# Routing attention of a two-layer kernel: keys on partitions for 512 queries at a time, split factors, the row maximum from its own pass

## The chip, the cores and the metric

The kernel runs on one core of a Trainium2 chip. Its metric is the device time of one execution in microseconds (us). TensorE (PE, with its weight loads PEld), VectorE (DVE), ScalarE (ACT), GpSimd (POOL) and SyncE (SP, here a DMA queue) run their own instruction streams in order and wait for each other by semaphores.

## What is computed

A tensor x of 2048 rows by 256 and a context of 1601 rows by 192 go through two layers. The first is a routing layer of one head; the second is a transformer block with self-attention (16 heads of 16), cross-attention to the same context and an MLP. The change touches the first layer:

```
tok    = context @ W_proj + b_proj                  # 1601 x 256
scores = x @ tok.T / sqrt(256)                      # 2048 x 1601
attn   = softmax(scores, axis=-1)
routed = attn @ tok                                 # 2048 x 256
ps_n, in_n = ln(x), ln(routed)
u = sigmoid([ps_n, in_n] @ W_u + b_u)
r = sigmoid([ps_n, in_n] @ W_r + b_r)
cand = tanh([r * ps_n, in_n] @ W_n + b_n)
x = ln((1 - u) * x + u * cand)
```

## The kernel before

x stands as 16 tiles of 128 rows; a chunk is four tiles (512 rows). The context has 13 key tiles, the last of 65 rows. The program has four parts in time.

**First stage** (list `stage1`). TensorE makes tok twice from ctxT, by features (`tokF`, L778) and by keys (`tokT`, L782), and the keys (`k`) and values (`v`) of the cross-attention; `norm` sums the squares of the keys by head (L753). ScalarE takes k units in three passes (`split`, L614 to L616), VectorE makes their low part (`lower_parts`, L1217).

**Routing loop** (function `l0` on each engine). Tile i has its scores made with queries on partitions: XT is the stationary operand, tokF moves, 16 recorded TensorE instructions into four PSUM banks (L827). VectorE reduces the maximum (L1323), ScalarE takes one exp over 1601 columns with its row sum (L652). TensorE turns the 13 blocks of the result (L859), ScalarE copies them out (L666), TensorE multiplies by tokT (L836). Then come per tile: the norm of the routed row and of x, a chain of about twenty short VectorE instructions (L1332 to L1349); four transposes (L869); reset and update gates (L845, L848); the candidate (L877); the blend and the output norm (L1356 to L1195); and the first norm of the second layer with two transposes (L796). In step i the loop does scores of tile i, the routed product of i-1, the gates of i-2, the output norm of i-3 and the transposes of i-4. It has 20 steps.

**Projections.** Once four tiles have passed, `qkv(stage3[n])` makes q, k and v of the self-attention for chunk n (L813, L810, L753). The tables `DENSE` and `WITHIN` put it: chunks 0, 1 and 3 run as a block of their own after steps 7, 11 and 19; chunk 2 is spread within steps 16 and 17.

**Attentions.** Self- and cross-attention with the MLP (L989 scores, L713 exp, L1006 values) follow. They start when chunk 3 is projected. Their stacked q and k parts are typed F32R: a value is split in a rounded high part and a low part, and a product of F32R operands is one recorded TensorE instruction, where one of f32 operands is two.

## Time and profile before

| | us |
|---|---|
| three runs | 1571.6, 1568.4, 1571.73 |
| their median | 1571.6 |
| the profiled execution, own time | 1572.35 |
| its span, first to last instruction | 1570.7 |
| TensorE busy | 1468.8 (94%) |
| ScalarE busy | 1072.1 (68%) |
| VectorE busy | 536.5 (34%) |
| TensorE share of the chain that ended last | 75% |

Busy time is the union of an engine's instructions. Ends of matmuls are modelled, so a distance between starts tells the pace and a duration the latency. The profiled execution is 0.75 us over the median of the runs.

### The profile page before, as it was taken

The numbers are of one execution on the slowest core, as the hardware profiler recorded it, in microseconds if no ns is written. First come the engines' busy times: TensorE is split into PE (matmuls) and PEld (weight loads), VectorE is DVE, ScalarE is ACT, GpSimd is POOL, SyncE is SP. The second block draws the span as 40 slices with busy tenths as digits, with TensorE's granted clock in tenths as the row PEclk, the third lists the DMA queues.
The fourth block names the chain that finished last, engine by engine and source line by source line (L and its number), as shares of the span: only waits on it lengthen the run. The fifth ranks groups of instructions, "written<-read, shape, count | busy, mean of one in ns | idle before, by whom it ended". The sixth has DMA issues, their size and how long they took to land.

```text
span 1570.7 us, 20677 instructions
## 1 busy us (share of the span) xinstructions
PE 1468.8 (94%) x8094; PEld 644.5 (41%) x8094; DVE 536.5 (34%) x1296; ACT 1072.1 (68%) x1297; POOL 41.7 (3%) x58
## 2 busy tenths in 40 slices
PE   8889989999867999999999999899999999999998
PEld 5467757757632222322322322232232432332346
DVE  1535545545553022230331332233232142133222
ACT  2323333333325999999999999798788797788852
POOL 2100000000001000000000000000000000000000
PEclk9999999999968999999999999899899999999999
DMA  7400010010016800010010056401000100000000
GB/s 218 171 7 7 8 57 19 8 67 5 31 53 125 139 22 11 11 40 22 11 38 13 19 77 115 102 19 61 13 12 11 35 12 11 18 18 1 2 13 14
DMA packets 36651, 64.22 MB, mean 41 GB/s; under 512 B 6464, under 2 KB 22656, under 8 KB 35808
## 3 DMA queue, kind: packets, MB, share of 16 engines
q1 hardware_dynamic: 31184, 41.40, 12.1%
q0 software_dynamic: 5360, 21.37, 3.8%
q8 instruction: 70, 1.15, 0.3%
q14 instruction: 37, 0.30, 0.1%
HBM read 40.85 MB, written 22.02 MB: 40 GB/s over the span
## 4 chain that ended last, share of the span: by engine, by line
PE 75%; ACT 17%; DVE 4%; issue 3%; DMA 1%; POOL 0%; DVEq 0%; SPq 0%; ACTq 0%; POOLq 0%
PE PS L1006 22%; PE PS L989 16%; ACT PX L713 14%; PE PS L827 6%; PE PS L836 6%; PE PS L1057 4%; PE PS L1067 3%; PE PS L1042 2%; PE PS L778 2%; PE PS L877 2%; PE PS L813 2%; PE PS L753 2%; PE PS L845 1%; PE PS L848 1%; PE PS L782 1%
## 5 line engine op out<-in xcount | busy, mean ns | idle before, releaser
L713 ACT ACTIVATE PX<-PS 128x1024 f32<-128x1024 f32 (+1 forms) x928 | 883.8, 1040 | 138.6 <-PE PS L989 87.4
L1006 PE MATMUL PS<-PX,V 128*32 128x512 f32 (+1 forms) x3712 | 501.0, 612 | 5.0 <-ACT PX L713 3.1
L989 PE MATMUL PS<-QST,stack 50*128 50x512 f32 (+1 forms) x1856 | 386.0, 473 | 20.0 <-issue 14.0
L989 PEld LDWEIGHTS PS<-QST,stack 50*128 50x128 f32 (+1 forms) x1856 | 156.3, 186 | 421.7 <-ACT PX L713 340.2
L1006 PEld LDWEIGHTS PS<-PX,V 128*32 128x32 f32 (+1 forms) x3712 | 74.1, 109 | 152.3 <-issue 126.9
L1448 DVE COPY OT<-PS 128x512 f32<-128x512 f32 x32 | 22.1, 692 | 309.6 <-PE PS L1006 308.3
L652 ACT ACTIVATE PR<-PS,small 128x1601 f32<-128x1601 f32 x16 | 25.5, 1596 | 117.0 <-DVE small L1324 117.0
L827 PE MATMUL PS<-tokF,XT 128*128 128x512 f32 (+1 forms) x256 | 93.2, 518 | 4.2 <-DVE small L1305 3.6
L836 PE MATMUL PS<-tokT,PT 128*128 128x256 f32 (+1 forms) x416 | 93.3, 382 | 0.6 <-DVE CZ L1374 0.6
L836 PEld LDWEIGHTS PS<-tokT,PT 128*128 128x128 f32 (+1 forms) x416 | 78.0, 191 | 10.6 <-issue 0.8
L659 ACT ACTIVATE TR<-PS,small 128x128 f32<-128x128 f32 x32 | 10.0, 363 | 85.8 <-PE PS L848 85.8
L827 PEld LDWEIGHTS PS<-tokF,XT 128*128 128x128 f32 x256 | 45.7, 193 | 53.3 <-issue 53.2
L1067 PE MATMUL PS<-W,HIDT 128*128 128x256 f32 x192 | 52.0, 418 | 9.8 <-ACT HIDT L699 9.8
L1057 PE MATMUL PS<-HC,W 128*128 128x512 f32 x96 | 53.2, 641 | 0.0
L1475 DVE RECIPROCAL REC<-REC 128x256 f32<-128x256 f32 x30 | 52.6, 1753 | 1.0
L1067 PEld LDWEIGHTS PS<-W,HIDT 128*128 128x128 f32 x192 | 36.9, 202 | 34.6 <-issue 30.0
L1323 DVE TENSOR_REDUCE small<-PS 128x1 f32<-128x1601 f32 x16 | 29.2, 1826 | 53.6 <-PE PS L827 53.6
L1520 DVE TENSOR_SCALAR HIDT<-PS,cols 128x512 f32<-128x512 f32 x24 | 18.0, 751 | 79.9 <-PE PS L1057 79.8
L1498 DVE TENSOR_TENSOR XH<-PS,rows 128x256 f32<-128x256 f32 x28 | 11.9, 425 | 81.6 <-PE PS L1042 81.6
L859 PE MATMUL PS<-ident,PR 128*128 128x128 f32 (+1 forms) x208 | 30.8, 290 | 8.6 <-ACT PT L666 4.7
L614 ACT ACTIVATE PARTS<-PS,cols 128x512 f32<-128x512 f32 (+1 forms) x16 | 10.3, 642 | 40.7 <-PE PS L778 24.7
L813 PE MATMUL PS<-hF,SAW 128*128 128x512 f32 x64 | 32.9, 652 | 4.4 <-ACT hF L635 4.4
(146 smaller groups left out, 1187.4 us busy)
## 6 DMA issues: line engine op xcount, KB each, us to landing
QST<-q_parts SPq DMA_DIRECT2D x192, 64.0 KB
q_parts<-PARTS POOLq DMA_DIRECT2D x16, 512.0 KB, 3.4
stack<-k_parts SPq DMA_DIRECT2D x24, 200.1 KB, 6.8
stack<-k_parts SPq DMA_DIRECT2D x18, 256.0 KB
k_parts<-KPARTS POOLq DMA_DIRECT2D x8, 512.0 KB, 3.2
v_cross<-V POOLq DMA_DIRECT2D x1, 3328.0 KB, 10.0
V<-v_cross SPq DMA_DIRECT2D x2, 1664.0 KB, 13.0
k_parts<-PARTS POOLq DMA_DIRECT2D x6, 512.0 KB, 3.2
```

Of the source, the lines that this page charges most:

```text
L713: act.activation(PX[0:kr, (2 * t + half) % 4, :, :], PS[0:kr, slot:slot + 2, :], ACT.Exp, scale=SCALE).then_inc(at["exp"], 1)
L753: ins = pe.matmul(PS[0:HEADS, bank, 0:w], headsum[:, mm, :], SQ[:, mm, 0:w], start=(mm == 0), stop=(mm == 1))
L778: ins = pe.matmul(PS[:, bank, 0:w], lhs, ctxT[:, c, n:n + w], start=(c == 0), stop=(c == 1))
L813: ins = pe.matmul(PS[:, u % 4, :], SAW[:, "qk".index(kind), c, mm * P:(mm + 1) * P], hF[:, c, n:n + w], start=(c == 0), stop=(c == 1))
L827: ins = pe.matmul(PS[:, b, 0:w], XT[:, par, c, :], tokF[:, c, n:n + w], start=(c == 0), stop=(c == 1))
L836: ins = pe.matmul(PS[:, 6, 0:D], PT[0:kr, kt, :], tokT[0:kr, kt, :], start=(kt == 0), stop=(kt == LT - 1))
L877: ins = pe.matmul(PS[:, 6, 0:D], RPS[:, c, :] if c < 2 else CF[:, par, c, :], W0[:, 2, c, :], start=(c == 0), stop=(c == 3))
L989: ins = pe.matmul(PS[0:kr, 2 * (n % LOOK) + jj, :], KST[a][lo:lo + NROW, pair, kt * P:kt * P + kr].bitcast(F32R), QST[lo:lo + NROW, pair, ...
L1006: ins = pe.matmul(PS[32 * j:32 * j + 32, 6, :], V[0:kr, kt, 2 * (g // 2 * GH + j) + g % 2, :], PX[0:kr, (2 * t + j // 2) % 4, j % 2, :], s ...
L1057: ins = pe.matmul(PS[:, 7, :], (CAWQ if kind == "u" else W1)[:, c, i * P:(i + 1) * P], HC[:, c, :], start=(c == 0), stop=(c == 1))
L1067: ins = pe.matmul(PS[:, 7, 0:D], HIDT[:, k, i * P:(i + 1) * P], W2[:, k, :], start=(k == 0), stop=(k == HID // P - 1))
L1475: ch(ve.reciprocal(part, part))
```

## The change

Scores are now made with keys on partitions, for 512 queries at a time, from the raw context: x is multiplied by W_proj first (`q_unit`), giving 192 features (the bias of tok adds the same to every key of a row and falls out of the softmax). The query features and the context are split in high and low F32R parts (QP; CHI and CLO; CN by keys). Per key tile, `l0_scores` is five F32R matmuls of 512 columns and `l0_pv` six, into two banks that gather over the 13 key tiles; the result stands by context features and is multiplied by W_proj per tile (`route`, f32, which also brings the row sum in a column of its own). tokF, tokT and the 13 transposes per tile are gone. ScalarE takes exp twice per key tile (`exps`), to F32R and to f32, and VectorE makes the low part (`lower`). The row maximum is needed ahead of the exp and comes from a pass of its own: 16 pieces per chunk (`max_piece`, two F32R matmuls of high parts alone, 128 queries by up to 512 keys), a VectorE maximum for each (`max_taken`), turned to a row (`max_rows`) and put in as one more feature.

The loop is now one of slots: `slot(k)`, 23 of them. In slot k of the first 16 stand three key tiles of chunk k // 4 (four if k is a multiple of 4, j = 0), a share of the maxima of the next chunk (none at j = 0, which has the next chunk's `q_unit` instead), and the tile work for tiles k-4 (route, hats), k-5 (gates, candidate), k-6 (finish) and k-7 (transposes). Slots 16 to 22 have tile work alone, and the projections of chunks 1 and 2 within slots 16, 17, 19 and 20.

```diff
-    stage1 = ([("tokF", n, w, mm) for n, w in pcs for mm in range(2)] + [("tokT", kt, 0, 0) for kt in range(LT)])
+    stage1 = [("v", kt, 0, 0) for kt in range(LT)]
     for i, (n, w) in enumerate(pcs):
         stage1 += [("k", n, w, mm) for mm in range(2)]
-        stage1 += [("v", kt, 0, 0) for kt in range(LT * i // len(pcs), LT * (i + 1) // len(pcs))]
+        stage1 += [("max", i * len(pcs) + p, 0, 0) for p in range(len(pcs))]
         stage1 += [("norm", i, w, 0)]
     stage1 = numbered(stage1)
...
-    DENSE = {2 * TPC - 1: 0, 3 * TPC - 1: 1, 5 * TPC - 1: 3}
-    WITHIN = {TILES: stage3[2][:MIDDLE], TILES + 1: stage3[2][MIDDLE:]}
...
+    DENSE = {10: 0, 22: 3}
+    WITHIN = {16: stage3[1][:MIDDLE], 17: stage3[1][MIDDLE:], 19: stage3[2][:MIDDLE], 20: stage3[2][MIDDLE:]}
+    SLOTS = TILES + TPC + 3
...
+    def max_share(k):
+
+        j = k % TPC
+        if j == 0 or k // TPC + 1 >= CHUNKS:
+            return []
+        first = (k // TPC + 1) * TPC * len(pcs)
+        return [first + m for m in ((0, 1, 2, 3, 4, 5), (6, 7, 8, 9, 10, 11), (12, 13, 14, 15))[j - 1]]
```


TensorE, the new functions and the slot:

```diff
+        def max_piece(m):
+
+            b, tt, p = m // (TPC * len(pcs)), m // len(pcs) % TPC, m % len(pcs)
+            n, w = pcs[p]
+            w += w % 2
+            if m == 0:
+                pe.wait_ge(S["ctx_hi"], len(CTX_PARTS))
+            if m % (TPC * len(pcs)) == 0:
+                pe.wait_ge(S["l0_q_hi"], 2 * b + 2)
+            bank, q = max_bank(m), QP[b % 2]
+            take(bank, S["l0_max_taken"], m + 1)
+            pe.matmul(PS[:, bank, 0:w], q[:, 0, tt * P:(tt + 1) * P].bitcast(F32R),
+                      CHI[:, 0, n:n + w].bitcast(F32R), start=True, stop=False)
+            pe.matmul(PS[:, bank, 0:w], q[0:HALF, 3, tt * P:(tt + 1) * P].bitcast(F32R),
+                      CHI[0:HALF, 1, n:n + w].bitcast(F32R), start=False, stop=True).then_inc(S["l0_max"], 1)
+
+        def max_rows(b):
+
+            pe.wait_ge(S["l0_negmax"], b + 1)
+            take(rows_bank(b), S["l0_shift"], b + 1)
+            for tt in range(TPC):
+                ins = pe.matmul(PS[SUM:SUM + 1, rows_bank(b), tt * P:(tt + 1) * P], sm(NEGM + tt), ident[:],
+                                start=True, stop=True)
+            ins.then_inc(S["l0_rows"], 1)
+
+        for mm in range(2):
...
+            if kt == 0:
+                pe.wait_ge(S["l0_q_lo"], 2 * b + 2)
+                pe.wait_ge(S["l0_shift"], b + 1)
+            take(n % 2, S["l0_exp"], n + 1)
+            out_ = PS[0:kr, n % 2, :]
+            pe.matmul(out_, CHI[:, 0, keys].bitcast(F32R), q[:, 0, :].bitcast(F32R), start=True, stop=False)
+            pe.matmul(out_, CHI[:, 0, keys].bitcast(F32R), q[:, 1, :].bitcast(F32R), start=False, stop=False)
+            pe.matmul(out_, CLO[:, 0, keys].bitcast(F32R), q[:, 0, :].bitcast(F32R), start=False, stop=False)
+            pe.matmul(out_, CHI[:, 1, keys].bitcast(F32R), q[:, 2, :].bitcast(F32R), start=False, stop=False)
+            pe.matmul(out_, CLO[0:SUM + 1, 1, keys].bitcast(F32R), q[0:SUM + 1, 3, :].bitcast(F32R),
+                      start=False, stop=True).then_inc(S["l0_scores"], 1)
...
+            pe.wait_ge(S["l0_lo"], n + 1)
+            if first:
+                for bank in (4, 5):
+                    take(bank, S["l0_oc"], b + 1)
+            hi, lo = PH[0:kr, n % RING, :].bitcast(F32R), PL[0:kr, n % RING, :].bitcast(F32R)
+            for bank, f, w in ((4, 0, P), (5, P, SUM + 1)):
+                c_hi, c_lo = (CN[0:kr, kt, o + f:o + f + w].bitcast(F32R) for o in (0, CW))
+                pe.matmul(PS[0:w, bank, :], c_hi, hi, start=first, stop=False)
+                pe.matmul(PS[0:w, bank, :], c_lo, hi, start=False, stop=False)
+                ins = pe.matmul(PS[0:w, bank, :], c_hi, lo, start=False, stop=last)
+            ins.then_inc(S["l0_pv"], 1)
...
+        def route(i):
+
+            b, tt = divmod(i, TPC)
+            if i == 0:
+                pe.wait_ge(S["wn_loaded"], 32)
+            pe.wait_ge(S["l0_oc"], b + 1)
+            wait(pe, S["l0_hat"], i)
+            pe.matmul(PS[:, 6, 0:D + 1], OC[:, 0, tt * P:(tt + 1) * P], WN[:, 0, :], start=True, stop=False)
+            pe.matmul(PS[:, 6, 0:D + 1], OC[0:SUM + 1, 1, tt * P:(tt + 1) * P], WN[0:SUM + 1, 1, :],
+                      start=False, stop=True).then_inc(S["l0_routed"], 1)
...
+                l0_scores(n)
+                if more:
+                    q_unit(b + 1, 0)
+                l0_pv(n - 2)
+                l0_scores(n + 1)
+                l0_pv(n - 1)
+                if g is not None:
+                    gates(g)
+                if more:
+                    q_unit(b + 1, 1)
+                l0_scores(n + 2)
+                l0_pv(n)
+                if r is not None:
+                    route(r)
+                l0_scores(n + 3)
+                if g is not None:
+                    candidate(g)
+                l0_pv(n + 1)
+                if r is not None:
+                    hats(r)
+                if h is not None:
+                    h_transposed(h)
+                return
+            ms = max_share(k)
+
+            def maxima(i):
+
+                if i < len(ms):
+                    max_piece(ms[i])
+                elif ms and i == 4:
+                    max_rows(b + 1)
+
+            l0_scores(n)
+            maxima(0)
+            l0_pv(n - 2)
+            if r is not None:
+                route(r)
+            maxima(1)
+            l0_scores(n + 1)
+            maxima(2)
+            l0_pv(n - 1)
+            if g is not None:
+                gates(g)
+            maxima(3)
+            l0_scores(n + 2)
+            maxima(4)
+            l0_pv(n)
+            if r is not None:
+                hats(r)
+            if g is not None:
+                candidate(g)
+            if h is not None:
+                h_transposed(h)
+            maxima(5)
```


ScalarE and VectorE:

```diff
+            kr = key_rows(1, n % LT)
+            act.wait_ge(S["l0_scores"], n + 1)
+            if n == 0:
+                act.wait_ge(S["v_cross_stored"], 16)
+            wait(act, S["l0_pv"], n + 1 - RING)
+            act.activation(PH[0:kr, n % RING, :].bitcast(F32R), PS[0:kr, n % 2, :], ACT.Exp, scale=SCALE0)
+            act.activation(PEXP[0:kr, n % RING, :], PS[0:kr, n % 2, :], ACT.Exp, scale=SCALE0) \
+                .then_inc(S["l0_exp"], 1)
+
+        def routed_out(b):
+
+            act.wait_ge(S["l0_pv"], LT * (b + 1))
+            wait(act, S["l0_routed"], TPC * b)
+            act.copy(OC[:, 0, :], PS[:, 4, :])
+            act.copy(OC[0:SUM + 1, 1, :], PS[0:SUM + 1, 5, :]).then_inc(S["l0_oc"], 1)
...
+            ins.then_inc(S["l0_q_lo"], 1)
+
+        def max_taken(m):
+
+            p = m % len(pcs)
+            ve.wait_ge(S["l0_max"], m + 1)
+            ve.tensor_reduce(sm(MXP + m % (TPC * len(pcs))), PS[:, max_bank(m), 0:pcs[p][1]], AX, ALU.max) \
+                .then_inc(S["l0_max_taken"], 1)
+
+        def negmax(b):
+
+            ve.wait_ge(S["l0_max_taken"], (b + 1) * TPC * len(pcs))
+            ve.tensor_reduce(sm(NEGM, TPC), sm(MXP, TPC * len(pcs)).rearrange("p (t n) -> p t n", t=TPC), AX, ALU.max,
+                             negate=True).then_inc(S["l0_negmax"], 1)
...
+        def lower(n):
+
+            kr = key_rows(1, n % LT)
+            ve.wait_ge(S["l0_exp"], n + 1)
+            ve.tensor_tensor(PL[0:kr, n % RING, :].bitcast(F32R), PEXP[0:kr, n % RING, :], PH[0:kr, n % RING, :],
+                             ALU.subtract).then_inc(S["l0_lo"], 1)
...
+            if j == 0:
+                more = b + 1 < CHUNKS
+                lower(n)
+                if more:
+                    q_lo(b + 1, 0)
+                lower(n + 1)
+                gates(g)
+                if more:
+                    q_lo(b + 1, 1)
+                lower(n + 2)
+                norms(r, f, h)
+                finish(f)
+                candidate(g)
+                lower(n + 3)
+                if k == 0:
+                    x_stats()
+                return
+            ms = max_share(k)
+
+            def maxima(i):
+
+                if i < len(ms):
+                    max_taken(ms[i])
+                elif ms and i == 4:
+                    negmax(b + 1)
+
+            lower(n)
+            maxima(0)
+            norms(r, f, h)
+            maxima(1)
+            maxima(2)
+            lower(n + 1)
+            gates(g)
+            finish(f)
+            maxima(3)
+            if j == TPC - 1:
+                maxima(4)
+            lower(n + 2)
+            if j < TPC - 1:
+                maxima(4)
+            candidate(g)
+            maxima(5)
```


SyncE loads the context in two parts of three DMAs each, the cross-attention weights, WQ and 512 columns of xT ahead of the context by keys (CN32, 1601 rows of 193 values) and the constants; each later xT chunk is one DMA. The key quarters of the self-attention, which two steps of the loop loaded before, are all loaded once slot 19 has routed tile 15. GpSimd sets ones in V a second time, after the last product of the routing, since the new tiles PH and PL lie there.

TensorE in the loop, before: one tile, from its routed product to the next tile's scores.

```order
L836 MATMUL PS<-tokT,PT 128x256 x13
L845 MATMUL PS<-CF,W_96 128x128 x8
L848 MATMUL PS<-W_96,CF 128x256 x4
L859 MATMUL PS<-ident,PR 128x128 x12
L859 MATMUL PS<-ident,PR 65x128
L869 MATMUL PS<-ident,XHS 128x128 x4
L877 MATMUL PS<-W_96,RPS 128x256 x2
L877 MATMUL PS<-W_96,CF 128x256 x2
L796 MATMUL PS<-ident,XH_97 128x128 x2
L827 MATMUL PS<-tokF,XT 128x512 x6
```


The same place in the change (slot 11; QP_87 and QP_88 are the two chunks' query parts):

```order
L1062 MATMUL PS<-CF,W_100 128x128 x8
L1065 MATMUL PS<-W_100,CF 128x256 x4
L928 MATMUL PS<-CHI,QP_88 128x66
L930 MATMUL PS<-CHI,QP_88 128x66
L1009 MATMUL PS<-QP_87,CHI 65x512
L1010 MATMUL PS<-QP_87,CHI 65x512
L1011 MATMUL PS<-QP_87,CLO 65x512
L1012 MATMUL PS<-QP_87,CHI 65x512
L1013 MATMUL PS<-QP_87,CLO 65x512
L938 MATMUL PS<-ident,small 1x128 x4
L1029 MATMUL PS<-PH,CN 128x512
L1030 MATMUL PS<-PH,CN 128x512
```


The transposes of PR are gone. Between gates and candidate now stand a key tile's scores (five rows), a piece of the next chunk's maximum (L928, L930), the turned maxima (L938) and a key tile's product.

VectorE in the same place, before: from the update gate to the next tile's maximum.

```order
L1356 TENSOR_TENSOR UZ<-PS,rows_90 128x256
L1360 TENSOR_SCALAR RPS<-TR 128x256
L1361 TENSOR_TENSOR RPS<-RPS,CF 128x256
L1366 TENSOR_SCALAR E_103<-E_103,small 128x256
L1367 TENSOR_TENSOR E_103<-E_103,rows_90 128x256
L1368 TENSOR_TENSOR X<-E_103,rows_90 128x256
L1193 BN_STATS small<-X 128x6
L1195 BN_AGGR small<-small 128x2
L1374 TENSOR_TENSOR CZ<-PS,rows_90 128x256
L1379 TENSOR_TENSOR E_103<-CD,X 128x256
L1380 SCALAR_TENSOR_TENSOR E_103<-TU,E_103 128x256
L1382 SCALAR_TENSOR_TENSOR E_103<-E_103,X 128x256
```


And in the change (slot 9), from the last instruction of the norms:

```order
L1646 TENSOR_SCALAR XH_102<-X,small 128x256
L1532 TENSOR_REDUCE small<-PS 128x1 x2
L1625 TENSOR_TENSOR PL<-PEXP,PH 128x512
L1655 TENSOR_TENSOR UZ<-PS,rows_99 128x256
L1657 TENSOR_SCALAR RPS<-TR 128x256
L1658 TENSOR_TENSOR RPS<-RPS,CF 128x256
L1666 TENSOR_SCALAR E_108<-E_108,small 128x256
L1667 TENSOR_TENSOR E_108<-E_108,rows_99 128x256
L1668 TENSOR_TENSOR X<-E_108,rows_99 128x256
L1457 BN_STATS small<-X 128x6
L1459 BN_AGGR small<-small 128x2
L1532 TENSOR_REDUCE small<-PS 128x1
```


The reduction over 1601 columns, one a tile, is gone from its place; three pieces of maximum and a low part stand among the tile work in this stretch.

TensorE after the last routed tile, before (steps 17 to 19 and chunk 3's projections begin):

```order
L845 MATMUL PS<-CF,W_96 128x128 x8
L848 MATMUL PS<-W_96,CF 128x256 x4
L813 MATMUL PS<-hF,SAW 128x512 x2
L810 MATMUL PS<-SAW,hF 128x256 x4
L753 MATMUL PS<-SQ,headsum 16x512 x2
L877 MATMUL PS<-W_96,RPS 128x256 x2
L877 MATMUL PS<-W_96,CF 128x256 x2
L796 MATMUL PS<-ident,XH_97 128x128 x6
L813 MATMUL PS<-hF,SAW 128x512 x4
L810 MATMUL PS<-SAW,hF 128x256 x4
```


And in the change (slots 20 to 22, the same projections begin):

```order
L993 MATMUL PS<-hF,SAW 128x512 x2
L990 MATMUL PS<-SAW,hF 128x256 x4
L893 MATMUL PS<-SQ,headsum 16x512 x2
L1062 MATMUL PS<-CF,W_100 128x128 x8
L1065 MATMUL PS<-W_100,CF 128x256 x4
L1072 MATMUL PS<-W_100,RPS 128x256 x2
L1072 MATMUL PS<-W_100,CF 128x256 x2
L975 MATMUL PS<-ident,XH_102 128x128 x6
L993 MATMUL PS<-hF,SAW 128x512 x4
L990 MATMUL PS<-SAW,hF 128x256 x4
```


The order within a slot is turned: projections now stand ahead of the gates. Ahead of these rows there are four more slots of tile work without scores, where the loop before had one step.

## Rows read from the trace of the kernel before

**Rows 1.** Windows of stages: us, busy us (x) of PE, PEld, DVE, ACT, POOL, clock, DMA, GB/s.
```profile
62.00:132.60 70.60, 61.66 (x271) 44.19 (x272) 34.69 (x124) 20.56 (x43) 0.39 (x1) 0.95 0.15 57
132.60:231.00 98.40, 90.94 (x413) 64.39 (x412) 55.37 (x157) 35.51 (x78) 2.89 (x4) 1.00 0.08 27
231.00:329.60 98.60, 91.05 (x413) 64.53 (x413) 53.07 (x151) 34.99 (x76) 2.90 (x4) 1.00 0.10 32
329.60:410.60 81.00, 76.68 (x373) 58.05 (x373) 44.88 (x135) 26.76 (x62) 0.00 (x0) 1.00 0.03 10
410.60:490.70 80.10, 53.23 (x184) 31.78 (x185) 42.92 (x131) 22.91 (x47) 6.83 (x10) 0.83 0.21 72
490.70:1570.70 1080.00, 1040.56 (x6260) 349.26 (x6260) 288.22 (x559) 912.97 (x958) 15.47 (x26) 0.97 0.16 34
```

**Rows 2.** Chain of waits by time, one tile of the routing: start us, us, what.
```profile
132.59 5.54 PE PS L827 x16
138.13 5.67 PE PS L836 x26
143.80 1.79 PE PS L845 x16
145.58 1.74 PE PS L848 x8
...
150.56 1.85 PE PS L877 x8
152.62 5.54 PE PS L827 x16
```

**Rows 3.** Timeline of TensorE in that tile: start, us, line, out<-in, shape, count, idle.
```profile
149.93 0.63 PE L869 MATMUL PS<-ident,XHS 128*128 128x128 f32 x4 [0.61 <-ACT PT L666]
...
152.24 0.38 PE L796 MATMUL PS<-ident,XH 128*128 128x128 f32 x2
```

**Rows 4.** Timeline of VectorE in that tile.
```profile
143.91 0.16 DVE L1332 RECIPROCAL small<-small 128x1 f32<-128x1 f32 x1 [3.66 <-PE PS L836]
...
149.14 0.42 DVE L1356 TENSOR_TENSOR UZ<-PS,rows 128x256 f32<-128x256 f32 x1
...
150.39 0.41 DVE L1366 TENSOR_SCALAR E<-E,small 128x256 f32<-128x256 f32 x1
...
152.66 0.42 DVE L1374 TENSOR_TENSOR CZ<-PS,rows 128x256 f32<-128x256 f32 x1
...
155.69 0.18 DVE L1195 BATCH_NORM_AGGREGATE small<-small 128x2 f32<-128x6 f32 x1
```

**Rows 5.** Groups by form: busy us, mean ns of one, idle before.
```profile
L1217 DVE TENSOR_TENSOR PARTS<-PARTS 128x512 fp32r<-128x512 f32 x14 | 9.7, 693 | 30.1 <-ACT SQ L616 30.1
...
L615 ACT ACTIVATE PARTS<-PS,cols 128x512 fp32r<-128x512 f32 x14 | 9.6, 683 | 0.0
```

**Rows 6.** Timeline of TensorE where three score pairs of self-attention stand together.
```profile
740.94 0.96 PE L989 MATMUL PS<-QST,stack 50*128 50x512 f32 x6
```

**Rows 7.** Page, part 5: all score matmuls of the attentions.
```profile
L989 PE MATMUL PS<-QST,stack 50*128 50x512 f32 (+1 forms) x1856 | 386.0, 473 | 20.0 <-issue 14.0
```

**Rows 8.** Window of the first loads.
```profile
3.00:13.00 10.00, 6.25 (x8) 2.67 (x9) 0.00 (x0) 0.98 (x3) 4.80 (x1) 1.00 1.07 253
```

**Rows 9.** Chain by time, one key piece of the first stage.
```profile
32.60 3.43 PE PS L778 x8
...
38.62 1.82 PE PS L753 x4
40.44 3.63 PE PS L778 x8
```

**Rows 10.** Timeline of VectorE, statistics of x after the first tile.
```profile
69.98 5.33 DVE L1279 BATCH_NORM_STATS2 small<-X 128x6 f32<-128x256 f32 x16
```

**Rows 11.** Timeline of TensorE after the last tiles.
```profile
462.97 0.66 PE L796 MATMUL PS<-ident,XH 128*128 128x128 f32 x2 [4.37 <-DVE XH L1349]
...
490.70 1.65 PE L989 MATMUL PS<-QST,stack 50*128 50x512 f32 x6 [5.18 <-issue]
```

706 lines of the change are left out of this document (414 added, 292 removed).

## The prediction

> **What bounds the kernel now.** I read the windows of the stages first: the routing, with the first stage and the projections, takes the first 490.7 us, and the attentions the 1080 us behind, which the change leaves as they are [rows 1]. In the loop TensorE is busy 91 to 95% of each window, at full clock but for the start; in the stretch from 410.6 to 490.7, where tiles drain and chunk 3 is projected, only 53.2 of 80.1 us [rows 1]. The chain of waits then gives the tile: from its start at 132.59 to the next at 152.62 are 20.03 us, of it 5.54 scores, 5.67 routed product, 3.53 gates, 1.85 candidate [rows 2], the rest transposes, hats 0.5 and two of the next norm 0.2 to 0.3 among them [rows 3], with short waits for copies. VectorE is no bound today: its tile work runs from 143.91 to 155.87, 12.0 us: norms 5.2 (143.91 to 149.14), gate inputs 1.25, finish 2.3, candidate and blend 3.2 [rows 4]. But each of these pieces waits for TensorE or is waited for by it, and that decides what a faster product is worth.
>
> So an amount of TensorE work taken out helps where TensorE sets the pace, and not where the loop through TensorE, ScalarE and VectorE does.
>
> **The price of an F32R matmul.** The trace has them in pairs that share the array. Three pairs take 0.96 us from the first start to the last end [rows 6], one lasts 0.473 [rows 7]: (0.96 - 0.47) / 2 = 0.245 us from pair to pair. A full-width f32 instruction of 256 columns, with a 128-column weight load for each, takes 5.67 / 26 = 0.22 [rows 2]. No row has a full-width F32R of 512 columns. From below: half an f32 instruction of 512 columns, which is 3.43 / 8 = 0.43 [rows 9], gives 0.215; from above 0.96 / 3 = 0.32, the last end counted in [rows 6]. I take 0.22, nearest to the full-width row, and 0.1 more (0.32 less 0.22) for the first of a group that waits for a semaphore. The Trainium skill (TensorE: Matmul & The Clock Gate, Step-by-step and LDWEIGHTS) says a weight load is pulled ahead of running matmuls only if the row groups don't conflict or it goes to the background buffer, and that 128 columns take about 107 ns. If all 668 wide ones paid that, an estimate by that page, 71 us would come on top. The pairs above lie on the same rows as the pair before and run at 0.245, which speaks against most of it.
>
> **First stage.** Out: 16 tokF and 26 tokT units' worth of TensorE, about 25 us. In: 3.4 us `q_unit`, 16 pieces of maximum. But it starts later: WQ and 512 columns of xT stand behind a larger context part and weights, 2.35 MB where a first start needed 0.6 MB. At 253 GB/s [rows 8] that is 9.3 us plus issue and landing, so TensorE begins near 12.5 instead of 6.75. `q_unit` runs at the slow first pace (8 instructions in over 6.25 us [rows 8]), to 19.4, the v units to 31.5. A key piece is then bound by a chain: k units 3.4, the split on ScalarE (three passes, 0.68 each and some 0.6 from start to start, twice), the low parts and four maxima in VectorE's order (0.69 each, 0.6 to 0.65 from start to start) [rows 5], TensorE's norm 1.8: 9.2 us, against 40.44 less 32.60, 7.84, before with three v units in it [rows 9]. Three are 27.6, the short one 4.5; the first lowers of CN hide under the split. Then two subtractions of 1601 columns (about 3.7 on VectorE) stand ahead of the first scores, nothing hides them. Sum 67.5 against 62.0: **+5.5**.
>
> **Chunk 0** (no tile work yet). 13 key tiles of 11 matmuls and 24 wide and 8 narrow ones of the maximum are 167 x 0.22 + 0.9 = 37.6; `q_unit` 3.4, `max_rows` 1, 42 groups that wait 4: 46. The statistics of x (5.33 for the first part [rows 10], about 9 with the rest) stand on VectorE behind slot 0, and its maxima and low parts behind them; some 6 of these show, at a slower clock for a while. 52 against 70.6 [rows 1]: **-18.6**.
>
> **Chunk 1 and 2, full slots (j = 1 to 3).** TensorE alone would need 3 x 1.2 scores, 3 x 1.4 product, 2.3 maxima, 0.9 route, 6.4 tile work [rows 2, 3] = 17.4. The loop is longer. Counted from VectorE's fourth maximum, which frees bank 3 for the hats: hats 0.5, candidate 1.85, transposes 0.3, a wait of 0.7 for ScalarE to take bank 2, scores 1.2, maximum 0.45, product 1.4, route 0.9, maximum 0.45, scores 1.2, maximum 0.45, product 1.4, gates 3.5, reset on ScalarE 0.85, then on VectorE gates 1.25, finish 2.3 [rows 4], maximum 0.6: 19.3 us. At j = 0 the products (5.6), scores (4.8), q (3.4) and 6.4 tile work are 20.2, and the route stands so late that hats wait for the norms (5.2): 22. The turned maxima at j = 3 make TensorE wait for VectorE, 2 more. 22 + 3 x 19.3 + 2 = 82 for chunk 2; chunk 1 is still filling (no gates in slot 4, no finish in 5) and takes 75. Chunk 1 before took 98.4 with a block of projections, now within the tail: **-23.4**. Chunk 2: 98.6 before [rows 1], 82 + 18.4 now (the block of projections is 98.4 less 4 x 20.03, some 18.4): **+1.8**.
>
> **Chunk 3.** No maxima, no q: three slots by TensorE, 3 x (3.6 + 4.2 + 0.9 + 6.4) = 45.3, and a first one of 19 where hats wait: 64 against 81.0: **-17**.
>
> **The tail.** Slots 16 to 22 have no scores to fill them. VectorE's order paces: norms 5.2, gates, finish, candidate 6.8 make 12 at least for slots 16 to 18 and 19; with projections and the wait for the last copies 24, 15, 12, 17.5, 13 for slots 16 to 20, then 5.1 and 3 (TensorE waits 4.4 us for that norm alone today [rows 11]). 90, and from there to the first score of self-attention as now, 1.65 + 26.1 (462.97 to 490.7 [rows 11]): 118 against 80.1: **+38**. Clock: in that stretch the granted clock is 0.83 on average today [rows 1], which is time at the lower of the two levels, 1.2 GHz, and the tail now is longer and as thin; I have put nothing on top, since VectorE is the pace there.
>
> **DMAs.** xT is four loads instead of sixteen. The key quarters are issued after slot 19, 12 issues beside 55 us of tail and projections; without that cover each 0.5 us issue would show. GpSimd's second memset stands ahead of the stores of chunk 1's parts, which nobody needs before the tail's end.
>
> Sum: 5.5 - 18.6 - 23.4 + 1.8 - 17 + 38 = -13.7 us, to 1558.7 against 1572.35. The profiled execution is 0.75 above the median; I say **1559**.
>
> **Rivals.** (1) *The slots fall to TensorE's own sum*: VectorE runs ahead and the waits overlap. Six full slots gain 1.9, the two first ones 2, chunk 1's and 2's rows wait 2 less, tail 6: about -25 more, 1534. For it: VectorE has slack on average, 55 of 98 us busy [rows 1]. Against: in-order queues, and PSUM banks 2 and 3 each have two or three users. (2) *Slower: the full-width F32R loads its weights exposed*, 0.32 for each of 668. That is 67 us, of which slack in VectorE-paced stretches hides a quarter: 1559 + 50 = 1609; at 0.28, 1585. It decides from 0.02 above my 0.22 (13 us, the whole gain). For it: 0.245 and 0.32 are what the pairs show; against: the 0.22 of the f32 rows. (The Trainium skill's rule above would be this case.) (3) *Slower: the tail and slots wait longer*: each of 12 slots with tile work ending on another engine by 2 us, 24 us: 1583. (4) *No change*: halves of these, 1569 to 1575. That the change doesn't do what it says can be left out: the instruction order shows it.
>
> **Chances.** Forecast, 1545 to 1568: 0.36. Rival 1: 0.18. Same: 0.10. Rival 2: 0.15. Rival 3: 0.21. A measurement of this kernel can tell 0.2% (3 us) from nothing. Faster 0.54, same 0.10, slower 0.36. Gains and losses both hold much; the forecast's own range is 1545 to 1568, and the range for all is 1532 to 1592, which leaves out the ends of rivals 1 and 2.
>
> **What would show it.** First scores (the new L1009) near 67.5; in chunks 1 and 2 five or six L1009 to L1013 and L1029 to L1031 rows at 0.22 each (0.32 says rival 2); start of slot 8 to slot 12 near 100, of it 18.4 projections; TensorE idle in full slots some 2 us, ended by VectorE's maximum (L1532) or ScalarE; from the last key tile to the first score of self-attention 118. The forecast is wrong if the loop's full slots last 17.5 or 22, or the tail 105 or 135. The attentions must keep 1080.

## The result: 1.4% slower, where 0.8% faster was forecast

The changed kernel takes 1593.55 us (median of 4 runs, 1591.8 to 1597.88), the kernel before 1571.66 beside it: a ratio of 1.0144, 95% interval 1.0121 to 1.0168. The forecast of 1559 missed, and so did its range of 1545 to 1568; the result lies 1.6 us outside even the range for all rivals, 1532 to 1592. The profiled execution has a span of 1590.1 us and a mean clock of 0.961.

Windows of the changed kernel, cut at the first scores of each chunk, where TensorE is through with slot 15 (3.5 us behind the last scores) and at the first score of self-attention (columns as in [rows 1]):

```profile
11.00:77.10 66.10, 58.45 (x148) 23.11 (x148) 28.51 (x50) 21.92 (x37) 6.40 (x9) 0.92 0.66 227
77.10:133.10 56.00, 50.49 (x179) 31.32 (x180) 27.51 (x76) 16.37 (x30) 0.00 (x0) 0.91 0.03 10
133.10:212.40 79.30, 73.14 (x323) 51.15 (x321) 46.28 (x136) 26.96 (x59) 0.00 (x0) 0.98 0.02 7
212.40:320.90 108.50, 97.63 (x403) 65.30 (x400) 63.63 (x175) 38.52 (x84) 2.86 (x4) 0.94 0.05 20
320.90:383.40 62.50, 60.70 (x314) 49.05 (x312) 47.12 (x145) 28.68 (x68) 0.00 (x0) 1.00 0.00 1
383.40:508.35 124.95, 90.06 (x344) 55.73 (x342) 80.35 (x246) 42.00 (x91) 13.11 (x15) 0.87 0.19 70
508.35:1590.10 1081.75, 1038.68 (x6260) 347.30 (x6260) 288.74 (x560) 912.70 (x958) 15.38 (x26) 0.98 0.16 33
```

Set against the prediction, stage by stage (the last column is what the kernel that came out of the experiments takes, b1 below):

| stage, us | before | forecast | after | b1 |
|---|---|---|---|---|
| first scores at | 62.0 | 67.5 | 77.1 | 66.1 |
| chunk 0 | 70.6 | 52 | 56.0 | 43.9 |
| chunk 1 | 98.4 | 75 | 79.3 | 73.4 |
| chunk 2 | 98.6 | 100.4 | 108.5 | 99.7 |
| chunk 3 | 81.0 | 64 | 62.5 | 62.8 |
| tail | 80.1 | 118 | 125.0 | 124.2 |
| attentions | 1080.0 | 1080 | 1081.8 | 1082.2 |

The error of 33 us (the profiled execution took 1591.8, the forecast's sum was 1558.7) is not in one place: 9.6 in stage 1, 4.0, 4.3 and 8.1 in the three chunks that have maxima to find, 7 in the tail. Chunk 3, the only one without maxima, was forecast 1.5 too long. That pointed to the maxima. TensorE's timeline in a slot of chunk 2 (start, us, line, out<-in, shape) shows them among the other F32R products:

```profile
301.65 0.39 PE L1010 MATMUL PS<-QP,CHI 128*128 128x512 f32 x1
301.88 0.39 PE L1011 MATMUL PS<-QP,CLO 128*128 128x512 f32 x1
302.11 0.39 PE L1012 MATMUL PS<-QP,CHI 128*128 128x512 f32 x1
302.34 0.39 PE L1013 MATMUL PS<-QP,CLO 65*128 65x512 f32 x1
302.57 0.39 PE L928 MATMUL PS<-CHI,QP 128*128 128x512 f32 x1
302.89 0.49 PE L930 MATMUL PS<-CHI,QP 64*128 64x512 f32 x1
303.31 0.50 PE L1029 MATMUL PS<-PH,CN 128*128 128x512 f32 x1
303.66 0.40 PE L1030 MATMUL PS<-PH,CN 128*128 128x512 f32 x1
```

From start to start the scores go at 0.23 us, the one over 65 rows too. The product over 64 rows (L930) starts 0.32 behind its neighbour, the next 0.42 behind it, and the one after that 0.35 (303.31 to 303.66). Over all 64 pieces the median from start to start is 0.33 behind L928 and 0.42 behind L930, against 0.23 for each line of the scores and values but their first.

In stage 1 the chain of waits has something else too, a store of keys for which ScalarE waits before it may fill the buffer again:

```profile
40.49 8.79 DMA k_parts<-PARTS
49.28 0.02 issue
...
49.44 0.69 ACT PARTS L671
```

and in the chunks TensorE's list of waits (us in total, times, longest) for 133 to 321 us is led by the shift row, made from the maxima, with the last maximum before it:

```profile
PE PS L938 <- DVE small L1538: 6.3, 2, 3.1
PE PS L928 <- ACT hF L722: 3.7, 1, 3.7
```

### The profile page after: what moved, and what is told of

It is laid out like the page before. It is cut to its first block, busy times and chain, and to the rows that moved or that the text cites. A ratio compares the mean times of both kernels' runs of the same rounds, so it can differ in the third digit from the quotient of the medians.

```text
span 1590.1 us, 20571 instructions
## 1 busy us (share of the span) xinstructions
PE 1469.1 (92%) x7958; PEld 623.0 (39%) x7958; DVE 582.1 (37%) x1387; ACT 1088.4 (68%) x1328; POOL 46.4 (3%) x61
## 4 chain that ended last, share of the span: by engine, by line
PE 72%; ACT 16%; DVE 7%; issue 3%; DMA 1%; SPq 0%; DVEq 0%; POOL 0%; ACTq 0%; POOLq 0%
PE PS L1270 22%; PE PS L1253 16%; ACT PX L853 14%; PE PS L1321 4%; PE PS L1331 3%; PE PS L1306 2%; PE PS L1029 2%; PE PS L993 2%; PE PS L1062 2%; PE PS L1072 2%; PE PS L1065 2%; PE PS L893 1%; PE PS L1030 1%; PE PS L1031 1%; PE PS L1289 1%
## 5 line engine op out<-in xcount | busy, mean ns | idle before, releaser
L741 ACT ACTIVATE PH<-PS 128x512 fp32r<-128x512 f32 (+1 forms) x52 | 31.1, 598 | 96.7 <-PE PS L1013 96.5
L1331 PE MATMUL PS<-W,HIDT 128*128 128x256 f32 x192 | 51.5, 415 | 9.8 <-ACT HIDT L839 9.8
L757 ACT ACTIVATE TR<-PS,small 128x128 f32<-128x128 f32 x32 | 10.0, 364 | 62.8 <-PE PS L1065 62.8
L1029 PE MATMUL PS<-PH,CN 128*128 128x512 f32 (+1 forms) x104 | 47.3, 455 | 1.2 <-DVE PL L1625 1.2
L1625 DVE TENSOR_TENSOR PL<-PEXP,PH 128x512 fp32r<-128x512 f32 (+1 forms) x52 | 35.8, 688 | 32.1 <-ACT PEXP L742 31.6
L1030 PE MATMUL PS<-PH,CN 128*128 128x512 f32 (+1 forms) x104 | 42.8, 411 | 0.0
L1031 PE MATMUL PS<-PL,CN 128*128 128x512 f32 (+1 forms) x104 | 42.5, 409 | 0.0
L928 PE MATMUL PS<-CHI,QP 128*128 128x512 f32 x64 | 27.3, 426 | 14.1 <-DVE small L1532 10.3
L1532 DVE TENSOR_REDUCE small<-PS 128x1 f32<-128x512 f32 x64 | 35.1, 570 | 9.6 <-PE PS L930 8.7
L770 ACT ACTIVATE CF<-PS,cols 128x128 f32<-128x128 f32 x64 | 24.0, 453 | 18.5 <-PE PS L1050 18.5
## 6 DMA issues: line engine op xcount, KB each, us to landing
v_cross<-V POOLq DMA_DIRECT2D x1, 3328.0 KB, 10.9
V<-v_cross SPq DMA_DIRECT2D x2, 1664.0 KB, 13.1
```

Source lines behind the costliest of these rows:

```text
L1029: pe.matmul(PS[0:w, bank, :], c_hi, hi, start=first, stop=False)
L1030: pe.matmul(PS[0:w, bank, :], c_lo, hi, start=False, stop=False)
L1031: ins = pe.matmul(PS[0:w, bank, :], c_hi, lo, start=False, stop=last)
L1331: ins = pe.matmul(PS[:, 7, 0:D], HIDT[:, k, i * P:(i + 1) * P], W2[:, k, :], start=(k == 0), stop=(k == HID // P - 1))
L1532: ve.tensor_reduce(sm(MXP + m % (TPC * len(pcs))), PS[:, max_bank(m), 0:pcs[p][1]], AX, ALU.max) \
L1625: ve.tensor_tensor(PL[0:kr, n % RING, :].bitcast(F32R), PEXP[0:kr, n % RING, :], PH[0:kr, n % RING, :], ALU.subtract).then_inc(S["l0_lo"], 1)
```

## Experiments

Times are medians beside runs of the kernel before on the same chip, whose median was between 1572.1 and 1573.5; the ratio is to those. "Half clock" is the time before the first score of self-attention that the trace's clock records give at the lower of the two levels, 1.2 GHz: 69.4 us in the changed kernel, 33.8 in the one before. The stretch ahead of the first record (13 to 17 us in these two and in all variants of the changed kernel) is not counted.

One warning for the first stage: where its code is the same, its length still differs from trace to trace. The first score stands at 77.0 us in e1 and at 75.2 in e4, at 66.1 in b1 and at 68.4 in b2, so a difference of 2 us there, seen once, shows nothing by itself.

**e1_max128: the second product of a maximum piece over 128 rows** (it also waits for `l0_q_lo` in place of `l0_q_hi`).

```diff
-            pe.matmul(PS[:, bank, 0:w], q[0:HALF, 3, tt * P:(tt + 1) * P].bitcast(F32R),
-                      CHI[0:HALF, 1, n:n + w].bitcast(F32R), ...)
+            pe.matmul(PS[:, bank, 0:w], q[:, 2, tt * P:(tt + 1) * P].bitcast(F32R),
+                      CHI[:, 1, n:n + w].bitcast(F32R), ...)
```

> The second product of every maximum piece reads all 128 rows (the block of q whose rows 64 to 127 hold the low parts, against the rows of the context that lie there twice) in place of 64. Theory A, narrow rows: a product over 64 rows that stands beside products over 128 rows is what makes a wide piece of the changed kernel take 0.42 + 0.42 us from start to start; at full width both should go at 0.23. 48 wide pieces by 0.38 us is 18 us, less what is hidden behind waits: 12 to 17 us off the changed kernel's 1593.6, so 1577 to 1582, the chunks 0 to 2 of the routed layer 3 to 5 us shorter each. Theory B, three engines in a ring: TensorE's pieces only fill time in which it would wait for VectorE and ScalarE; then 0 to 4 us, 1590 to 1593.

Measured: 1579.19 (ratio 1.0051, 1.0034 to 1.0068), 14.4 less than the changed kernel. Chunks 0 to 2 are 51.5, 76.4 and 103.9, 12.0 less in sum; stage 1 stays at 77.0, since its pieces lie beside the wait for the store. The second product reads twice as many rows, and the piece takes 0.48 us (292.37 to 292.85) where it took 0.74; the product behind it is back at 0.23 too (median):

```profile
292.13 0.40 PE L1013 MATMUL PS<-QP,CLO 65*128 65x512 f32 x1
292.37 0.40 PE L928 MATMUL PS<-CHI,QP 128*128 128x512 f32 x1
292.61 0.40 PE L930 MATMUL PS<-CHI,QP 128*128 128x512 f32 x1
292.85 0.40 PE L1029 MATMUL PS<-PH,CN 128*128 128x512 f32 x1
```

Theory A holds (12 to 17 us were expected).

**e1b_both64: both products of a piece over 64 rows.** `q[0:HALF, 0, ...]` and `CHI[0:HALF, 0, ...]` in the first product too.

> The changed kernel with both products of a maximum piece over 64 rows (the first leaves out rows 64 to 127 of q, so the maxima are those of a part of the scores; the shift row stays a valid shift as far as they go). Theory A1, the pair 128 then 64 is what exposes the weight loads: inside a piece both products are narrow, so a piece's second product goes at 0.23 us, and only the step to and from the neighbours over 128 rows costs 0.3 to 0.4. Theory A2, every product over 64 rows is slow by itself: 0.42 + 0.42 us a piece stay, and the time with them, 1590 to 1595. By A1 a wide piece takes 0.55 to 0.7 us in place of 0.84 and the time is 1583 to 1589.

Measured: 1590.71 (1.0122, 1.0098 to 1.0146). In stage 1, where pieces stand in a row, a product over 64 rows behind another goes at 0.23:

```profile
48.67 0.39 PE L928 MATMUL PS<-CHI,QP 64*128 64x512 f32 x1
48.90 0.39 PE L930 MATMUL PS<-CHI,QP 64*128 64x512 f32 x1
```

So 64 rows are not slow; the step from 128 to 64 and back is (A1). But the time lies above A1's range and in that of A2 (two executions only), and the loop shows why:

```profile
303.81 0.39 PE L1013 MATMUL PS<-QP,CLO 65*128 65x512 f32 x1
304.12 0.49 PE L928 MATMUL PS<-CHI,QP 64*128 64x512 f32 x1
304.46 0.39 PE L930 MATMUL PS<-CHI,QP 64*128 64x512 f32 x1
304.77 0.51 PE L1029 MATMUL PS<-PH,CN 128*128 128x512 f32 x1
305.12 0.40 PE L1030 MATMUL PS<-PH,CN 128*128 128x512 f32 x1
305.35 0.39 PE L1031 MATMUL PS<-PL,CN 128*128 128x512 f32 x1
```

From start to start: 0.31, 0.34, 0.31, 0.35, 0.23. Each change of rows costs about 0.1 us at its own step and 0.1 at the step behind it, even where that one stays at 64 rows, which A1 had put at 0.23. Around a piece that is 0.4 us, as in the changed kernel (0.1 + 0.2 + 0.1 there), so nothing is gained in the loop: the chunks 0 to 2 have 242.8 us in sum against 243.8. Half clock is 74.2 us, 4.8 more than in the changed kernel.

**e7_before_128_64, e7b_before_padded, e13_before_127_65: the cut by itself, in the kernel before.**

```diff
-KC = CTX // 2
+KC = (128, CTX - 128)
```

with the loads cut alike and each product over its own rows (e7); the second part read over 128 rows, of which 64 are cleared in both operands (e7b); a cut into 127 and 65 (e13).

> The kernel before with one edit: its context matrices are cut into 128 and 64 rows in place of 96 and 96 (the same products, columns and results). The pure cost of the new cut in a kernel that has nothing else of the change. Theory A: 104 products of 256 columns (two layouts of the tokens, the values) go from 0.22 to 0.31 us, the wide ones from 0.43 to 0.5: stage 1 is 8 to 12 us longer, the rest the same, 1579 to 1585. Rival, the cut costs nothing and the changed kernel's 0.31 came from its loads or its neighbours: 1570 to 1574.

> The kernel before with its context matrices cut into 128 and 64 rows as in the run above, but the second part read over all 128 rows, of which 64 hold zeros in both operands (cleared by GpSimd first). Theory A, the rows read make the difference, through the exposed weight loads and through the clock, which stayed at its lower level until 80 us: the products go at 0.22 and 0.43 us again, the clock rises by 15 us, and the time is 1570 to 1577. Rival, the cut's loads (more transfers, and other sizes) or the memory's layout cost it: 1600 to 1616 as above.

> The kernel before with its context matrices cut into 127 and 65 rows: one row more in the second part than in the cut into 128 and 64 that took 1615.7 us, nothing else. Theory A3, the array is used in another arrangement for a product of at most 64 rows, and the change from one to the other exposes the loads: with 65 rows there is no such change, the products go at 0.22 and 0.43 us and the time is 1568 to 1577. Rival, any change of the number of rows from one product to the next costs: 1600 to 1620 as with 64.

Measured: 1615.7 (1.0287, 1.0263 to 1.0312), 1570.65 (0.9989, 0.9972 to 1.0006) and 1611.32 (1.0254, 1.0236 to 1.0272). The cut costs 43.6 us, and full rows, with the same cut and the same loads, give all of it back: it is the 64 rows. TensorE's timeline of e7, and the same work in e7b:

```profile
32.11 29.76 PE L784 MATMUL PS<-WPJ,ctxT 128*128 128x256 f32 x52
...
80.16 4.29 PE L780 MATMUL PS<-ctxT,CAKV 128*128 128x512 f32 x8
84.38 3.84 PE L784 MATMUL PS<-CAKV,ctxT 128*128 128x256 f32 x12
```

```profile
18.49 11.44 PE L788 MATMUL PS<-WPJ,ctxT 128*128 128x256 f32 x52
29.76 3.60 PE L784 MATMUL PS<-ctxT,CAKV 128*128 128x512 f32 x8
33.20 2.75 PE L788 MATMUL PS<-CAKV,ctxT 128*128 128x256 f32 x12
```

At full clock (behind 80 us) the narrow form costs 3.84 / 12 = 0.32 against 0.23 us; over the 168 products of the stage that is some 17 us, an estimate. The larger part is the clock: in e7 the first clock record of the trace comes at 80.0 us, in e7b at 8.9, and until then a 256-column product takes 29.76 / 52 = 0.57. (The windows view prints 1.00 where it has no record yet; the durations say otherwise.) TensorE was busy from 5.6 us on, with products of 128 and 64 rows in turn, until the four of the norm (128 rows, 76.7 to 80.2), within which the clock rose. It did not fall again in the same mix behind 80 us, nor did the mix of the values' products in the changed kernel (16.8 to 33.0 us, full clock from 15.6) bring it down. So in e7 the mix kept a low clock from rising; that it lowers a high one, no run shows. My 8 to 12 us had counted the slower steps alone.

e13 tells two things. Once its data are there, 127 and 65 rows run as 96 and 96 do:

```profile
82.79 2.76 PE L784 MATMUL PS<-CAKV,ctxT 127*128 127x256 f32 x12
...
87.30 3.71 PE L780 MATMUL PS<-ctxT,CAKV 127*128 127x512 f32 x8
```

so the limit lies between 64 and 65 rows, as A3 has it. Its time lies 34 us above A3's range, since the loads into 127 and 65 partitions crawl: TensorE's first product starts at 20.0 us, and it waits for data twice more. The window from 3 to 20 us (DMA share and GB/s last), of e13 and of the kernel before:

```profile
3.00:20.00 17.00, 0.02 (x1) 0.05 (x1) 0.00 (x0) 0.00 (x0) 4.80 (x1) 1.00 0.10 33
```

```profile
3.00:20.00 17.00, 13.26 (x24) 5.82 (x25) 0.00 (x0) 3.73 (x7) 4.80 (x1) 1.00 1.08 290
```

A share of 0.10 of 16 DMA engines is the work of fewer than two. Why they are slow was not tried.

**e2_kv128: keys and values of stage 1 over 128 rows too** (on top of e1; the weights' rows 64 to 127 cleared).

> The full-width maximum pieces, and in stage 1 the second contraction half of the cross attention's keys and values reads 128 rows too (the weights' rows 64 to 127 cleared to zero). Theory A, narrow rows: the 52 products of the values go from 0.31 to 0.22 us each (4.7 us), the keys' units of a wide piece from 0.53 to 0.44 a product (0.7 us a piece), so the first score stands 5 to 8 us earlier than in the kernel with full-width maxima alone (77.0 there), and the time is 1571 to 1574. Rival, the first stage goes by its loads and by the store of the values that stands ahead of the keys' stores: the values end earlier, but so little behind it moves that under 2 us come of it, 1577 to 1579.

Measured: 1574.48 (1.0016, 1.0002 to 1.003), 4.7 below e1. The first score stands at 70.2 in place of 77.0; chunks 0 and 1 give 1.4 and 0.9 back. Theory A again: the first score moved as expected, the time is 0.5 us above its range.

**e3_values_store_sp, e10_store_later: the 3.3 MB store of the values** (both on top of e1). e3 has SP issue it; e10 leaves it to GpSimd, behind the second key piece:

```diff
+            if i == 1:
+                gp.dma_start(vd, V[:, 0:LT]...).then_inc(S["v_cross_stored"], 16)
```

and loads the gates' weights (1.5 MB) after the first score.

> The full-width maximum pieces, and the store of the cross attention's values (3.3 MB, 10.9 us) issued by SP in place of GpSimd, so that the keys' stores don't queue behind it. If that place in GpSimd's queue is what made ScalarE wait 8.1 us before the second piece of the keys, the first score stands 3 to 5 us earlier (77.0 before), 1574 to 1577. Rival: the two transfers share the same 16 DMA engines, the keys' stores take as much longer as they start earlier, and the stage keeps its length within 1 us: 1578 to 1580.

> The full-width maximum pieces, and the store of the cross values moved in GpSimd's queue behind the stores of the keys' second piece, the loads of the gates' weights moved behind the first score. Theory, the two transfers (4.8 MB) filled the DMA engines' rate just when the first keys' store needed it: that store takes 3 to 4 us in place of 8.6, the first score stands 3 to 6 us earlier (77.0 with full-width maxima alone), 1573 to 1576. Rival, the store then meets the third and fourth pieces' stores, and these wait in its place: 77 to 78, 1578 to 1581.

Measured: e3 1580.41 (1.005, 1.0033 to 1.0067), first score at 76.3: nothing; its keys' store still took 9.57 us. e10 1577.15 (1.0024, 1.0012 to 1.0036), first score at 74.5, 2.5 before that of e1 but only 0.7 before that of e4, whose stage 1 is e1's. In e10's chain the wait behind the first piece is gone and a shorter one has come up behind the third:

```profile
60.33 0.53 issue
60.85 5.86 DMA k_parts<-PARTS
```

So the place in the queue is innocent. What the first keys' stores lacked was the rate: from 35 to 50 us the changed kernel moves 349 to 426 GB/s, at a DMA share of 0.99 to 1.05, and they take 8.7 and 8.8 us; in e10 the same stretch moves 70 GB/s and they take 3.3 and 3.2. Both theories of e10 are half right: the wait moved, and the time lies between their ranges.

**e4_rows_behind: the products of the shift row behind the values' products** (on top of e1).

```diff
             l0_pv(n)
+            if j == TPC - 1 and ms:
+                max_rows(b + 1)
```

> The full-width maximum pieces, and the four products that turn the maxima into the shift row for the next chunk go behind the values' products of the same key tile (1.4 us of work) in place of ahead of them. If TensorE's wait of 3.1 us there for VectorE's last maximum costs its length, 1.4 us go in each of the chunks 0 to 2 and less half clock behind it: 3 to 6 us, 1573 to 1576. Rival: the shift row is needed by the first scores of the next chunk, and its way over ScalarE then ends later by as much: 0 to 1 us, 1578 to 1580.

Measured: 1572.21 (1.0002, 0.9988 to 1.0016), 7.0 below e1, more than hoped: chunks 1 and 2 are 71.8 and 99.7, 4.6 and 4.2 less. Chunk 0 gained nothing (52.9 against 51.5). The two waits themselves, 6.8 us in e1, shrink only by 2.8:

```profile
PE PS L938 <- DVE small L1538: 4.0, 2, 2.0
```

For the rest the clock accounts, by an estimate: within the two chunks the time at the lower level is 3.4 us in place of 17.1 (53.5 in place of 63.5 up to the attentions; the stretches at 146 and 200 us are gone). At half pace 13.7 us less are worth up to 6.9, and with 2.8 that is 9.7, against 8.8 measured.

**e8_lows_early: VectorE's two lone blocks moved into stage 1** (on top of e1): `CLO`'s subtractions ahead of the second key piece, `bn_stats` of eight tiles each ahead of the third and fourth.

> The full-width maximum pieces, and two pieces of VectorE's work moved into its idle time of stage 1: the low part of the context (3.6 us, between the end of stage 1 and the first score) goes ahead of the second piece of the keys, and the 16 statistics of x (5.3 us, between two key tiles of chunk 0) go ahead of the third and fourth. If both lie on the path where they stand, stage 1 is 3 to 4 us shorter (77.0) and chunk 0 4 to 5 us (51.5), and less half clock follows: 1570 to 1573. Rival: stage 1 is bounded by VectorE where they go, which gives half of it back: 1574 to 1577.

Measured: 1574.78 (1.001, 0.9999 to 1.0021). Chunk 0 is 44.5, 7.0 less, but the first score stands 1.5 later (78.5) and half clock grew to 75.9. The time lies in the rival's range, and the chain of stage 1 now ends over the moved statistics (2.5 us, 69.7 to 72.4), as the rival says; the 1.5 us alone would show nothing. The statistics belong in chunk 0's gaps.

**e5_no_maxima: without the pass.**

> Leaves the pass of maxima out whole (TensorE's 64 pieces and VectorE's 64 reductions; the shift row is zero, made from a cleared tile, by the same later steps). It is worth what the pass costs. Of TensorE 48 x 0.84 + 16 x 0.55 = 49 us, of VectorE 48 x 0.50 + 16 x 0.12 = 26 us. If TensorE bounds chunks 0 to 2 (theory A) 35 to 45 us go: 1550 to 1558, and chunks 0 and 1 come near chunk 3's 62.5 less what its projections take. If the ring of three engines bounds them (theory B), what goes is nearer VectorE's share: 15 to 25 us, 1569 to 1578.

Measured: 1541.13 (0.98, 0.9784 to 0.9817): the pass costs 52.4 us by the medians (49.1 between the two profiled executions), as much as all its TensorE work. That is beyond both theories' ranges, on theory A's side; with the pass go also its waits and the slower steps around its pieces. The three chunks give 10.9, 13.1 and 19.3, stage 1 4.3:

```profile
72.80:117.90 45.10, 41.19 (x147) 28.24 (x148) 18.79 (x60) 16.37 (x30) 0.00 (x0) 0.85 0.04 12
117.90:184.10 66.20, 60.72 (x289) 46.44 (x289) 38.12 (x120) 26.95 (x59) 0.00 (x0) 0.97 0.03 9
184.10:273.30 89.20, 81.86 (x370) 58.42 (x369) 55.19 (x159) 38.31 (x84) 2.85 (x4) 0.98 0.06 24
```

**e6_no_context_low: three low-part products fewer in each key tile** (`CLO[:, 0]` in the scores, `c_lo` in the values).

> Leaves out the three products of each key tile that read the low part of the context (one of five of the scores, two of six of the values), so the scores and values lose precision; no work of another engine changes. 52 key tiles x 3 x 0.23 = 36 us of TensorE. TensorE as the bound of the four chunks (theory A): 28 to 36 us go, 1558 to 1566. Ring of three engines (theory B): each key tile still waits for its exponentials and their low part, 5 to 15 us go, 1579 to 1589.

Measured: 1577.72 (1.0028, 1.0009 to 1.0048), but with a wide spread (1568.1 to 1581.9), and the profiled execution (1569.15) is near its lower end. By the median 15.8 of the 36 us go, just above theory B's 5 to 15 and well below theory A's 28 to 36. In the profiled execution, of the 9 us taken in each chunk, 5.9, 4.3, 6.9 and, in chunk 3, 2.8 come off, 19.9 in all, an upper end. Half clock is 82.2. Neither theory alone: in that execution TensorE's work counts at a half to three quarters where maxima and tiles share the slots, in chunk 3 at a third.

**b1_combined, b2_combined_dense: what pays, together.** b1 is e2 with e4, e10, `CLO` subtracted in two parts inside stage 1, and the statistics of x spread over chunk 0 by ones and twos; b2 also computes chunk 1's projections in the loop (`DENSE = {10: 0, 14: 1, 22: 3}`).

> The changed kernel with full-width operands in maxima, keys and values, the shift row's products behind the values' products, the store of the cross values behind the stores of the second piece of keys (with the gates' weights loaded after stage 1), the low part of the context subtracted in two parts inside stage 1, and the statistics of x spread over chunk 0 by ones and twos. If the single gains add (14 for the maxima, 5 for keys and values, 7 for the shift row, 4 for the store, 5 for the statistics): 1593.6 - 35 = 1559, range 1554 to 1566, 6 to 18 below the kernel before. If they share one path they add to 25 only: 1568.

> The same, with the projections of chunk 1 computed in the loop (after the tile slot 14) in place of the drain. Theory T, the drain is bounded by the latency of the last tiles, and what stands in it of projections is on that path: chunk 3 is longer by 15 to 18 us, the drain shorter by 15 to 22, the sum 0 to 5 us shorter than without. Rival, the projections in the drain fill TensorE's waits and cost little there: chunk 3 is longer by 15 to 18, the drain shorter by 5 to 10, the sum 5 to 13 us longer.

Measured: b1 1555.41 (0.9905, 0.9883 to 0.9926), 38 below the changed kernel and 1% below the one before, inside the range for gains that add. Half clock is 45.2. b2 1564.15 (0.9955, 0.9937 to 0.9973): chunk 3 is 16.5 longer, the tail only 9.8 shorter (114.4). The rival holds, with 8.7 us in all (2.3 of them are stage 1, whose code is b1's): in the tail the projections fill TensorE's waits. Windows of b1's stage 1, chunks and tail:

```profile
11.00:66.10 55.10, 44.71 (x148) 24.70 (x149) 28.31 (x50) 21.50 (x37) 6.47 (x9) 0.97 0.69 245
66.10:110.00 43.90, 43.16 (x180) 31.05 (x180) 24.85 (x62) 16.38 (x30) 0.00 (x0) 0.96 0.15 48
110.00:183.40 73.40, 67.62 (x322) 52.07 (x322) 48.47 (x153) 27.11 (x59) 0.00 (x0) 0.98 0.02 8
183.40:283.10 99.70, 88.43 (x402) 63.78 (x401) 63.49 (x176) 38.57 (x84) 2.91 (x4) 0.98 0.05 22
283.10:345.90 62.80, 60.77 (x314) 49.12 (x313) 47.18 (x145) 28.72 (x68) 0.00 (x0) 1.00 0.00 1
345.90:470.10 124.20, 89.85 (x343) 55.91 (x342) 80.23 (x246) 42.07 (x91) 13.24 (x15) 0.87 0.19 70
```

## Why the prediction was wrong

**The price of a matmul.** "I take 0.22" was right for the full-width F32R product of 512 columns (0.23), and 0.1 more for the first of a waiting group too (L1009 has 0.33 in the median). The step that failed is its use for every product: each piece of maximum was costed as two full ones, 0.45, though the diff has `q[0:HALF, 3, ...]`. It takes 0.75 in place of 0.46, and the product behind it 0.1 more. All narrow products together are worth 19.1 us (e1 and e2), the largest part of the error. Rival 2 came nearest, with 0.1 more a product, but for all 668 wide products; only the 64 and their neighbours pay, and that its 1585 to 1609 holds the result is luck (its lower end, 0.06 by 668 less a quarter, would be 1589). That the 0.1 is an exposed weight load, as Rival 2 has it, was not shown: what fits it is that the same 0.1 comes on top at 256 and at 512 columns.

The trace of before did hold the price, where the prediction did not look. Inside a stage or a group the rows stay alike, 96 in the first stage, 50 in the attentions' scores [rows 6], but between groups they change. Two f32 products of 512 columns over 128 rows, with 50 rows behind them:

```profile
557.34 1.13 PE L1025 MATMUL PS<-SUMS,spread 128*128 128x512 f32 x2
558.40 0.73 PE L989 MATMUL PS<-QST,stack 50*128 50x512 f32 x4
```

They take 1.06 us, 0.53 each, where [rows 9] gives 0.43 (the first of the two may pay for a change of columns before it, 32 to 128). Likewise a product of that kernel's L1042 (256 columns, 128 rows) takes 0.31 where one over 50 rows follows (24 times) and 0.22 where one of its own line does.

**First stage, +9.6.** `q_unit` was done at 16.8, not 19.4, which gives 2.6. "The v units to 31.5" took 16.1 us in place of 12.1, from narrow rows; e2 gives 6.8 back for values and keys. The key piece of 9.2 us took 10.0 the first and third time (its narrow keys 4.2 in place of 3.4), but 13.8 the second: the step forgot the store that ScalarE waits for and what else is in transit then (e10: the store is 5.5 us shorter, the stage 0.7 to 2.5). The short piece and its maxima took 6.7 in place of 4.5. "About 3.7" for the two subtractions was right (3.5). With rows, store and subtractions mended, b1 reaches 66.1 and b2 68.4, against the 67.5 forecast.

**Chunk 0, +4.** The statistics of x, "some 6 of these show", show 11.2 us between two scores (93.9 to 105.0) in which about 4 of work would have fit; out of the way they give 7. b1 is 8 us below the forecast here.

**Chunks 1 and 2, +4.3 and +8.1.** With full rows they are 76.4 and 103.9, with the shift row's products moved 71.8 and 99.7, against 75 and 100.4. The loop count through three engines (19.3 a slot) was good. "2 more" for the turned maxima was too small: moving them alone is worth over 4 in each chunk, the larger part of it clock by the estimate under e4.

**Chunk 3, -1.5.** The time was right, the reason only in part: the prediction has its slots go "by TensorE", but of 9 us taken from TensorE there only 2.8 came off (e6).

**The tail, +7.** Slots 16 to 18 took 55.8 us (norms start at 410.3, 425.7 and 439.2) in place of 51, the rest to the last projections 43.2 in place of 38.6, and from there 26.0 in place of 27.8. The structure was right, and b2 shows that chunk 1's projections belong there. What the 9 us more in its first two parts are was not tried; VectorE's own work in it is 80.4 us here and 80.2 in b1, and the tail lasts 123 to 126 in all variants of the changed kernel but b2.

**Clock.** Time at the lower level before the attentions went from 33.8 to 69.4 us. For the tail, where the prediction says "I have put nothing on top", it is 31.9 against 27.0, the smaller part. The rest lies where the prediction has no term but "at a slower clock for a while": 10.2 us within stage 1 and 10.2 in chunk 0, 17.1 in the chunks 1 and 2, against none, 6.8 and none before. Each wait of a few us that the change put in front of TensorE (store, statistics, shift row) was costed at its length. In e4 waits shortened by 2.8 us came with chunks shorter by 8.8.

**Rivals 1 and 3.** Rival 1 (TensorE's own sum, 1534) is out: the time alone says so, and in e6 36 us less on TensorE gave 15.8. Rival 3 (longer waits, 24 us) is near in kind for what is not narrow rows, some 14 us, but these lie at a few places (store, statistics, shift row, tail), not as 2 us in each slot.

**Attentions.** 1081.8 against 1080, and 1079.3 to 1082.4 over the variants of the changed kernel, as expected.

## What to carry to other kernels

Price a matmul by its rows as well as its columns: an operand of 64 rows (or 50) among wider ones is a step in the stream, and reading duplicated or zeroed rows up to 128 is cheaper than leaving them out. A wait on TensorE's path can cost more than its length, in time at the lower clock, so a lone block of another engine's work (statistics, a big store, the last of a reduction) is to be cut up or moved before it is accepted. When a pass looks cheap by engine sums, take it out once: the maxima were 49 us of TensorE and cost about all of it, 52, where a ring of three engines would have hidden half.
